# Graph layer and expert feed-forward on one core: the node update spread over the edge steps

## The reference, cut to what matters

```python
def gnn(x, z, src, dst, sh, radial):            # x is the layer norm of the input
    s0, s1 = x0 @ W_sc0 * z, mix(x1, W_sc1) * z
    h0, h1 = x0 @ W_lin1_0 * z, mix(x1, W_lin1_1) * z
    w = silu(radial @ fc_w0) @ fc_w1            # 50000 x 256: wA, wB, wC, wD
    mid0 = [wA * h0[src] * sh0, wD * (h1[src] . sh1)]
    mid1 = [(wB * h0[src]) x sh1, wC * h1[src] * sh0]
    y0, y1 = segment_sum(mid0, dst), segment_sum(mid1, dst)
    return c_s * s + c_x * (y0 @ W_lin2_0, mix(y1, W_lin2_1)) * z
x = x + gnn(layernorm(x), ...)
n = layernorm(x)
x = x + gelu(n @ W1s + b1s) @ W2s + b2s         # shared expert, 256 -> 1024 -> 256
x = x + sum over the top 2 of 8 experts of weight_e * (gelu(n @ W1p[e] + b1p[e]) @ W2p[e] + b2p[e])
```

## Time and profile before

| what | value |
|---|---|
| median of three runs | 1195.45 us |
| the profiled execution's own time | 1192.31 us |
| its span in the trace | 1190.3 us |
| PE, PEld busy | 1043.2 (88%), 915.6 (77%) |
| DVE, ACT, POOL busy | 750.4 (63%), 727.2 (61%), 633.0 (53%) |
| mean granted TensorE clock | 0.971 of full speed |
| node stage, to the first gather | 0 to 60.6 us |
| edge stage, to the last add | 60.6 to 566.0 us |
| update stage, to the first shared matmul | 566.0 to 656.8 us |
| routed part, from its first matmul | 807.1 us to the end |

### The profile page before, as it was taken

How to read it: one execution, slowest core, us unless ns; L and a number is a source line. 1 busy time by engine, 2 the same in 40 slices (tenths; PEclk the granted TensorE clock), 3 DMA queues, 4 the chain that set the end, 5 groups by cost and what they waited for, 6 DMA issues and landing times. The chain is left out here.

```text
span 1190.3 us, 30949 instructions
## 1 busy us (share of the span) xinstructions
PE 1043.2 (88%) x8929; PEld 915.6 (77%) x8929; DVE 750.4 (63%) x1842; ACT 727.2 (61%) x2353; POOL 633.0 (53%) x645
## 2 busy tenths in 40 slices
PE   3788988889998988887688999988999999999991
PEld 2567777777777777776565999988999999899991
DVE  6566677766666667775476764445666656657561
ACT  3778888888888888886355645544444443444430
POOL 4077777777777777774000044442455455455552
PEclk9979999999999999999898999998999999999996
DMA  5233333343333433434554522323243444433221
GB/s 161 94 111 109 109 111 109 109 111 108 110 110 107 111 108 109 110 108 147 161 178 177 177 90 89 102 81 118 49 111 81 85 107 112 86 74 77 41 50 22
DMA packets 91911, 125.57 MB, mean 105 GB/s; under 512 B 29278, under 2 KB 70670, under 8 KB 91712
## 3 DMA queue, kind: packets, MB, share of 16 engines
q0 software_dynamic: 31792, 67.29, 22.9%
q1 hardware_dynamic: 56128, 54.01, 14.6%
q10 hardware_dynamic: 3920, 3.41, 0.8%
HBM read 98.30 MB, written 26.36 MB: 105 GB/s over the span
## 5 line engine op out<-in xcount | busy, mean ns | idle before, releaser
L568 ACT ACTIVATE hots<-hot,sh_st 128x64 f32<-128x64 f32 x1568 | 384.9, 334 | 0.2 <-issue 0.2
L711 PE MATMUL psY<-prod,hots 128*64 128x128 f32 x2352 | 279.4, 276 | 0.0
L707 PE MATMUL psY<-prod,hots 128*64 128x256 f32 x784 | 220.6, 401 | 52.1 <-DVE prod L615 52.1
L711 PEld LDWEIGHTS psY<-prod,hots 128*64 128x64 f32 x2352 | 256.0, 138 | 0.0
L543 POOL DMA_INDIRECT x_wlo<-h_tab,src_sb x224 | 214.2, 956 | 70.1 <-issue 70.1
L1738 ACT ACTIVATE q_hf<-q_psA,x_b 128x256 f32<-128x256 f32 x232 | 110.0, 474 | 191.9 <-PE q_psA L1282 186.5
L1683 POOL DMA_INDIRECT out_rows<-q_ob,q_index x58 | 119.9, 2068 | 136.1 <-DMA out_rows<-q_ob,q_index 89.2
L543 POOL DMA_INDIRECT rows<-h_tab,src_sb x168 | 161.0, 958 | 51.2 <-issue 51.2
L707 PEld LDWEIGHTS psY<-prod,hots 128*64 128x64 f32 x784 | 83.2, 136 | 91.0 <-DVE prod L615 89.4
L1282 PE MATMUL q_psA<-q_xhi,x_whi 128*128 x464 | 132.4, 285 | 9.4 <-DVE q_xlo L1776 9.0
L1869 PE MATMUL q_psB<-x_whi,q_hhi 128*128 128x256 f32 x464 | 133.0, 287 | 0.1
(11 more groups left out here) (212 smaller groups left out, 2281.2 us busy)
## 6 DMA issues: line engine op xcount, KB each, us to landing
x_raw<-in_w SPq DMA_DIRECT2D x18, 1024.0 KB, 5.8
x_wlo<-h_tab,src_sb POOLq DMA_INDIRECT x224
x_sb<-in_x SPq DMA_DIRECT2D x5, 640.0 KB, 5.4
h_tab<-x_sb ACTq DMA_DIRECT2D x5, 640.0 KB, 3.2
u_x<-in_x SPq DMA_DIRECT2D x5, 640.0 KB, 7.0
xnew_d<-u_x SPq DMA_DIRECT2D x5, 640.0 KB, 3.5
xn_d<-u_xn SPq DMA_DIRECT2D x5, 640.0 KB, 5.1
s_xnew<-xnew_d SPq DMA_DIRECT2D x5, 640.0 KB, 5.5
```

The source lines that it names most:

```text
L568: ins = nc.scalar.activation(hots[p][:, c, n, :], hot[p][:, c, :], ACT.Copy, scale=sh_st[p][:, 4 * c + n:4 * c + n + 1])
L707: nc.tensor.matmul(psY[p][0:SPAN, 0:FEAT], hots[p][:, c, 0, :], prod[p][:, c, 0:4, :].rearrange("p a u -> p (a u)"), start=(c == 0), stop= ...
L711: ins = nc.tensor.matmul(side[:, k::3 - k, :][:, 0:2, :], hots[p][:, c, k + 1, :], prod[p][:, c, 4::k + 1, :][:, 0:2, :], start=(c == 0 an ...
```

## The change

update_block is gone, and its work is in edge_block, in rounds of ITER = 8 steps with PAIR = 2 tiles of nodes. Rounds k = 0 and 1 are written out, k = 2 to 11 are a loop, and two steps follow. Round k of the loop puts at_work = k-1 (turn, mix, result) and done = k-2 (normalization, transposes, scores) at fixed steps q of it; the first turn_of below is PE's, the second DVE's. Tiles 22, 23 and 24 come after the last step.

```diff
+            def turn_of(r, k, q, done=None, at_work=None):
...
+                    hidden(r, k + (q + 2) // ITER, (q + 2) % ITER)
...
+                    radial(r, j + 1, (q + 1) % 2)
+                segment(r, j, q % 2)
+                if done is not None and q == 1:
+                    turn_x(r, done)
+                if done is not None and q == 3:
+                    score(r, done)
+                if at_work is not None and q == 3:
+                    turn(r, at_work * PAIR, y_st[:, 0:2, :])
+                if at_work is not None and q == 5:
+                    mix(r, at_work * PAIR)
+                    turn(r, at_work * PAIR + 1, y_st[:, 2:4, :])
+                if at_work is not None and q == 7:
+                    mix(r, at_work * PAIR + 1)
...
+            def turn_of(r, k, q, done=None, at_work=None):
...
+                    add_y(r, j - 2, q % 2)
...
+                    one_hot(r, j + 1, (q + 1) % 2)
+                if done is not None and q == 1:
+                    normalize(r, done)
+                products(r, k, j, q)
+                if done is not None and q == 0:
+                    graph_result(r, done, 1)
+                    variance(r, done)
+                if done is not None and q == 3:
+                    low(r, done)
+                if at_work is not None and q == 6:
+                    graph_result(r, at_work, 0)
```

variance takes the place of ACT's square root and DVE's reciprocal, with three Newton steps on both tiles, each operation waited for by the next:

```diff
+                for i in range(n):
+                    ins = nc.vector.bn_aggr(mv[:, i, :], stats[:, i, :])
...
+                step(nc.vector.tensor_scalar(var[:, few], mv[:, few, 1], EPS, None, ALU.add))
+                nc.vector.tensor_scalar(minus[:, few], var[:, few], -0.5, None, ALU.mult)
+                step(nc.vector.tensor_single_scalar(guess[:, few], var[:, few].bitcast(I32), 1, ALU.logical_shift_right))
+                step(nc.vector.tensor_scalar(guess[:, few], guess[:, few], -1.0, float(0x5F3759DF), ALU.mult, ALU.add))
+                y = guess[:, few].bitcast(F32)
+                for n_th in range(3):
+                    step(nc.vector.tensor_tensor(square[:, few], y, y, ALU.mult))
+                    step(nc.vector.tensor_tensor(square[:, few], square[:, few], minus[:, few], ALU.mult))
+                    step(nc.vector.scalar_tensor_tensor(out=rstd[:, few], in0=square[:, few], scalar=1.5, in1=y,
+                                                        op0=ALU.add, op1=ALU.mult))
```

ACT copies turned x (two copies 512 wide) at q = 2, the logits at q = 4 and the turned sums at q = 4 and 6. SP fetches a pair's sums to y_st and its base rows to x_st, stores rows and columns of the pair before, and waits for each; e_st now comes in chunks of four steps. To make room, psE and psW become single and the ring has four buffers:

```diff
-    RING = 7
+    RING = 4
...
-                pe.wait_ge(prod_done, (r * T + j) * 2 + 2 * RING - 2)
+                pe.wait_ge(prod_done, (r * T + j) * 2 + 2 * RING)
...
-        psE = [pb(f"psE{i}") for i in range(2)]
-        psW = [ctx.enter_context(nc.psum_tensor(f"psW{i}", [P, C, 4, MUL], F32)) for i in range(2)]
+        psE = pb("psE")
+        psW = ctx.enter_context(nc.psum_tensor("psW", [P, C, 4, MUL], F32))
+        psU, psO, psX = pb("psU"), pb("psO"), pb("psX")
```

In node_block, sh is loaded whole; POOL adds x to s tile by tile, SP stores the sum to base_d, and the last three tiles of it come back as x_end; the weights of the mix, and by ACT at the end those of expert 0, are loaded here. DVE compares each step's first node with a limit, 256 x (k-1), and asks for a second pass over all edges where one lies below it:

```diff
+                    pool.tensor_tensor(s_row[:, 0:MUL], s_row[:, 0:MUL], x_row[:, 0:MUL], ALU.add)
+                    pool.tensor_tensor(s_row[:, MUL:].rearrange("p (c u) -> p c u", c=3),
+                                       s_row[:, MUL:].rearrange("p (c u) -> p c u", c=3),
+                                       x_row[:, MUL:].rearrange("p (u c) -> p c u", c=3), ALU.add).then_inc(based, 1)
...
+            link(nc.vector.tensor_tensor(early[:], first_node[:], limit[:], ALU.is_lt))
```

xnew is now stored with its features in another order, so the shared block's last addition becomes two. ACT splits whi0 in round 1, DVE wlo0 after the last tile. The shared block begins with the first group of columns, and slots are written at 15 points of a group. In the routed part:

```diff
-            add(0, 0)
-            landed(0, 0)
-            add(0, 1)
-            with pool.Fori(1, all_but_two) as d:
-                rows_of(within(d + 4, TILES + 1))
-                landed(d - 1, 1)
-                add(d, 0)
-                landed(d, 0)
-                add(d, 1)
+            def adds(d, gather=None):
                 add(d, 0)
+                if gather is not None:
+                    rows_of(gather)
                 landed(d, 0)
                 add(d, 1)
+                landed(d, 1)
...
-                further(pe, n, first, lambda s, e=e: tile(s, e, (within(s - 1), e)))
+                further(pe, n, first, lambda s, e=e: tile(s, e, (within(s - 1), e), apart=e == EXPERTS - 1))
```

More of the change, by code:

```diff
@@ L385, in _ @@
             act.sem_inc(s_ready, 2)
+            for q in range(2):
+                act.sem_inc(h_out[q], 16)
             copy_columns(0, 0, 0)
@@ new lines, in copy_logits, with split @@
+            def copy_logits(r, p):
+                n = parts(p)
+                act.wait_ge(scored, r * (LAST + 1) + p + 2)
+                first = act.snap(p * PAIR) if not isinstance(p, int) else p * PAIR
+                nc.scalar.activation(logits[:, at(first, n), :].rearrange("p t e -> p (t e)"),
+                                     psO[:, FEAT:FEAT + n * EXPERTS], ACT.Copy).then_inc(logits_out, 1)
+            def split(r, i):
+                part = slice(PIECE * i, PIECE * (i + 1))
+                nc.scalar.activation(whi0[:, part], raw[:, part], ACT.Copy).then_inc(whi_part, 1)
@@ L654, in _ @@
                 one_hot(r, 0, 0)
-                one_hot(r, 1, 1)
-                products(r, 0, 0, 0, 0)
-                one_hot(r, 2, 0)
-                products(r, 0, 1, 1, 1)
-                def turn_of(r, k, q, last=False):
-                    j = k * TURN + 2 + q
-                    add_y(r, j - 2, q % 2)
-                    if not last:
-                        one_hot(r, j + 1, (q + 1) % 2)
-                    products(r, k * 2 + (2 + q) // RING, j, q % 2, (2 + q) % RING)
-                with dve.Fori(0, T // TURN - 1) as k:
-                    for q in range(TURN):
-                        turn_of(r, k, q)
@@ new lines, in _ @@
+            with pe.Fori(0, R) as r:
+                hidden(r, 0, 0)
+                hidden(r, 0, 1)
+                radial(r, 0, 0)
+                for q in range(ITER):
+                    turn_of(r, 0, q)
+                pe.wait_ge(w_ready, 1)
+                for q in range(ITER):
+                    turn_of(r, 1, q, None, 0)
+                with pe.Fori(2, ITERS) as k:
+                    for q in range(ITER):
+                        turn_of(r, k, q, k - 2, k - 1)
+                turn_of(r, ITERS, 0)
+                turn_of(r, ITERS, 1, ITERS - 2)
+                score(r, ITERS - 2)
+                pe.wait_ge(y_done, (r + 1) * T + 2)
+                pe.wait_ge(logits_out, r * (LAST + 1) + ITERS)
+                first = 2 * ITERS - 2
+                for t in range(first, NT):
+                    turn(r, t, y_sb[:, 2 * t:2 * t + 2, :])
+                    mix(r, t)
+                for p in range(ITERS - 1, LAST + 1):
+                    turn_x(r, p)
+                    score(r, p)
@@ L1803, in output, with tile @@
                                             None, ALU.mult).then_inc(ob_done, 1)
-            def tile(s, e, done=None, after=None):
+            def tile(s, e, done=None, after=None, early=None, late=None):
                 high(s, 0)
@@ L1813, in tile @@
                         output(*done)
+                    if f == 1 and early is not None:
+                        output(*early)
+                    if f == FC - 1 and late is not None:
+                        output(*late)
                     if f == 2:
@@ L1874, in down, with tile @@
                     ins.then_inc(down_done, 1)
[L1876 removed]
+            def tile(s, e, done=None, fresh=False, apart=False):
                 h = e % 2
@@ L1881, in tile @@
                     done_side = pe.snap(done[0] % 2)
+                if apart:
+                    for f in range(FC):
+                        down(*done, f, done_side)
                 for f in range(FC):
-                    if done is not None:
+                    if done is not None and not apart:
                         down(*done, f, done_side, fresh)
```

818 lines of the change are left out of this document (407 added, 411 removed).

## The result

The changed kernel takes 1258.4 us (median of four runs, 1254.6 to 1259.7) where the kernel before takes 1195.3: ratio 1.0522, 95% interval 1.0498 to 1.0546. It is 63 us slower, where 12 faster was forecast and 1222 was the end of the range. The profiled execution's span is 1256.9 us, 66.6 more than before, with a mean granted clock of 0.918 (before 0.971).

The account below looks back on a forecast made before the run. POOL's gather queue was taken to bound the edge stage, at 40.3 us per eight steps, with PE close behind. Terms +4 + 0 + 52 - 1 - 58 - 9 = -12 on 1195.45 gave 1183 us; range 1152 to 1222.

Parts of the forecast that it names:

- Last adds, -9: End of the routed part: reordered last expert leaves about one pair of adds less, -9 us (-4 to -14); moved gathers free.
- The rounds, +52: Ten loop rounds of the edge stage, each 45.5 us against 40.3, together +52 us (+24 to +73).
- the wait of PE: In each round, PE waits 4.1 us for DVE's products at q=1: DVE's 8.6 against PE's step of 4.46.
- the clock: In each round, the lower granted clock behind PE's wait costs 0.7 us, half of 1.4.
- The low end of the range: For the ten rounds, the cheapest case: a round of 42.7 us, +24 in all.
- Rival B: Edge rounds: PE's wait lowers the clock for a step's work, 4.46 us a round instead of 0.7; 1221 us; chance 0.22.
- Rival A, rounds free: Edge rounds: DVE's chain hides in its free time, the pace stays 40.3 us, total 1131; chance 0.12.
- Rival C: Edge stage: the new test adds a second pass over all edges, +505 us, total 1690; chance 0.01.
- The rest of the update, -58: From last add to first shared matmul: 33 us (28 to 38) remain of 90.8, saving 58.
- Two last steps: End of the edge stage: an eleventh variance chain costs +4 us; the table's forecast for the stretch is +3.
- Node stage: Start of the kernel: POOL's additions of s and x for 25 tiles cost +4 us (0 to +15).

Follow-up runs that it names:

- routed_old: The changed kernel with the whole routed part of the kernel before (order of adds, landings, gathers and last tiles); 1232.6 us, ratio 1.0316.
- last_tiles_old: The changed kernel with the last expert's order of before: down products interleaved with up products, outputs in the next tile; 1254.8 us, ratio 1.0505.
- no_root_b: The changed kernel with one operation in place of the twelve of the Newton root (inverse square root left out); 1216.3 us, ratio 1.0191.
- best1: The changed kernel with before's routed part, DVE's chain spread over the round, SP's fetches ahead of stores, expert 0's weights loaded in the first round; 1169.7 us, ratio 0.9794.

## Why the prediction was wrong, point by point

**Last adds, -9: wrong in sign, +32.5, and the largest miss (41.5 of 78.6).** The step that failed is the sentence that "the gathers moved between two adds lie in a wait of 4.6 and cost 1.3: nothing". I priced what they cost POOL and did not ask who waits for them. The gather of a tile must land before PE's transposes of it; it had stood behind nothing but the second add, and now stands behind the first add of the next tile, which waits for DVE's output and for a landing. 22.9 of the 32.5 are this order (routed_old against last_tiles_old; in the kernel before 22 by the times, 27.4 by the traces). The other 9.6 were read as apart, 4.9, and an open 4.7; the traces with and without apart lie too close for the first, so both stay open. The term itself was right as far as it went: behind the last product 11.8 are gone (26.5 to 14.7), 9.6 of them by apart, and I had put 10.8 less 2. What it left out is apart's own wait: with all down products first, PE needs the last low half at once, 5.9 and 4.9 us, and up to the last product apart cost what it gained.

**The rounds, +52: mechanism right, size short.** Ten of them cost +74 against ten of 40.3 (+70.1 in the table, where before's step 95 has the end's 3.9). A round went from 40.3 to 47.8, +7.5, forecast +5.2. Two terms of the sum were mis-sized. The first is the wait of PE, 5.1 and not 4.1: DVE's time between the two products is 11.1, not 8.6, with 1.12 for the mix that PE does behind the segment of q=7 and 1.21 before add_y, while PE has 6.0 us of work meanwhile (the rest of a mix and a hidden product more), not 4.46, which gives 1.5 back. The small operations were right: twelve in 2.4, 0.195 apart (forecast 0.19), the normalization 1.23 (1.24). The second is the clock, 2.5 and not 0.7; it was a value taken halfway. 47.8 - 5.1 - 2.5 = 40.2 is left for PE's own work, where 40.7 was put. What lies before add_y is open: its block number is read into a register from SBUF, and behind the waits of the chain DVE's queue may reach that read late. No run tried that; no_root_b shows only that the wait is 1.20 with one such operation too, and right behind products (409.55 in the same round, 346.99 in no_root_b) add_y starts with no wait. The low end of the range has a slip of its own: 35.7 + 5.0 + 3 with no clock term is 43.7, not 42.7, so +34 and not +24; the result lies at the other end.

**Rival B named the right place and way** (the clock behind the variance chain's wait), at too high a price: 2.5, not 4.46 a round. It put the turning point at a round of 46.7, and with 47.8 the kernel would have been slower without the routed part's loss too: routed_old is at 1.0316. I gave it 0.22, because 4.1 was shorter than the one wait of 5.36 with a fallen clock behind it; no_root_b shows a fall behind 2.86. The routed part has a smaller case of the same: 0.94 for 1.00 and 17.0 busy us more in the part where PE waits for rows and low halves. No term had that, and no run tried it by itself.

**Rival A, rounds free: refuted.** The 4.46 us step of the earlier trace rows is the changed kernel's too, three times in each round. PEld is busy 34.60 of 47.77 there, so the rule of the Trainium skill (Perfetto Trace Analysis, Identifying the Most-Contended Engine) that LDWEIGHTS busy time, next to the share of peak FLOPs, measures TensorE's headroom would still have left 13.2 us a round; the round grew by 7.5. best1's round shows it without the long wait: PEld 32.62 of 42.40, 77%, where PE waits for little more than 2 us. Rival C: one pass, 392 gathers.

**The rest of the update, -58: -52.** The stretch behind the last add is 38.8, not 33. SP's queue ends it as forecast, but starts later:

```profile
669.29 0.38 SPq L638 DMA_DIRECT2D xnew_d<-u_xnew  x1
...
677.36 0.55 SPq L652 DMA_DIRECT2D xT_d<-u_xhi  x1
...
680.75 0.36 SPq L638 DMA_DIRECT2D xnew_d<-u_xnew  x1
...
683.18 0.55 SPq L652 DMA_DIRECT2D xT_d<-u_xhi  x1
...
686.26 0.62 SPq L691 DMA_DIRECT2D cols_hi<-xT_d  x1
...
693.13 0.61 PE L1326 MATMUL s_psA<-cols_hi,x_whi 128*128 128x320 f32 x1 [12.95 <-ACTq L1464]
```

I had the last low half 16 behind the last add, the stores done at 22 and the first shared matmul at 33. DVE's timeline has the last low half (L935) end at 681.6, 27.2 behind; the stores are done at 31.9, when SP issues the load at 686.26, and the matmul comes at 38.8. So the step that failed is DVE's part, 11 longer, of which the last stores gave 1 back and the load and the start 4. Ahead of it stand pair 10's scores and columns, which I had left out, and the mixes of the last tiles run at the lower clock, 1.97 to 1.98 us each against the earlier trace rows's 1.09; and tile 24's result waits 3.16 more for the stores of pair 11.

**Two last steps, +9.2 for +3**: the eleventh chain costs a step of 10.6 us (11.15 in the loop), then the segment at the lower clock: DVE waits 4.80 for it ahead of the last adds.

**Node stage, +7.7 for +4.** POOL's additions take 0.33 and 0.66, 1.0 a tile: under the pace of 1.36. The estimate from the Trainium skill's figure (GPSIMD Engine Reference, Elementwise) was 0.6 to 0.9, a little short and on the right side. The block ends 3.7 later (the last group's store and its reload, the term I had). The other 4 are the start of the edge stage: the first e_st lands after 6.7 us where it took 2.6, and the first gather, for which the first products now wait, is issued 7.4 behind POOL's last set-up operation where it was 2.1. best1's trace has 3.1 of it gone with the weights' transfer moved.

## What to carry to other kernels

Work that fits an engine's free time on average can still cost its length if it sits in one gap of a loop, here one with single buffers (none was made double again to see what that part is): look at the free time of the gap, not of the round, and lay a dependent chain out in thirds over several gaps (59 us here, with nothing left out). The Trainium skill (Perfetto Trace Analysis, Optimization Strategy) says that the same gap coming back through a stretch can mean too few buffers; here 5.13 came back each round, and it went (to 1.23 and 0.78 in best1) with the buffers unchanged. When a transfer is moved in a queue, ask first who waits for its data, and behind whose waits it now stands; and if it was hiding a landing, what hides that landing now.

## What was not expected of the hardware

A wait of PE of 2.86 us was enough to bring the granted clock to 0.50 in the two us from 348 to 350; behind one of 5.13 it stayed there for 5 us and cost 2.5 a round. Thirty transposes a round, 3.5 us, that nobody reads won 18 us by keeping it up. The chip matters too: on one of those used the same kernel before took 1412.7 us, 1.18 times as long.
